# A typed graph-attention network on one core: table products on 32 rows, types loaded ahead, and the last part's orders skewed by groups

## The reference

```python
def gt_layer(x, ntype, etype, src, dst, Wk, Wq, Wv, Wa, Watt, Wmsg, pri, skip, g, b):
    k, q, v = (typed_linear(x, ntype, W).reshape(n, H, HS) for W in (Wk, Wq, Wv))
    kT = einsum('nhd,htdo->nhto', k, Watt)          # for every node, all 32 edge types
    vT = einsum('nhd,htdo->nhto', v, Wmsg)
    a = einsum('ehd,ehd->eh', kT[src, :, etype], q[dst]) * pri[:, etype].T / SQRT_D
    att = edge_softmax(a, dst, n)
    hag = segment_sum(vT[src, :, etype] * att[:, :, None], dst)
    h = silu(typed_linear(hag, ntype, Wa))
    alpha = sigmoid(skip[ntype])[:, None]
    return layernorm(h * alpha + x * (1.0 - alpha)) * g + b
h = x
for l in range(2): h = gt_layer(h, ...)
return layernorm(x + h @ ff_w + ff_b)
```

## Time and profile before

| | us |
|---|---|
| median of 3 runs | 6708.48 (6702.58 to 6715.25) |
| the profiled execution | 6708.81 |
| its span, first to last instruction | 6707.0 |
| table stage of layer 0, first to last copy | 518.5 to 1209.7 |
| table stage of layer 1, first to last copy | 3427.2 to 4220.0 |
| last part | 6394 to 6707 |

### The profile page before, as it was taken

The page is one execution under the profiler, slowest core; times in us unless marked ns, Lnnn a source line. Parts: engine busy times, 40 slices in busy tenths (PEclk is TensorE's granted clock), DMA queues, the critical chain, the costliest instruction groups (busy, mean ns, idle before and its releaser), DMA issues. The chain is left out here.

```text
span 6707.0 us, 77358 instructions
## 1 busy us (share of the span) xinstructions
PE 4184.1 (62%) x19359; PEld 2998.1 (45%) x19360; DVE 3641.0 (54%) x6709; ACT 1684.7 (25%) x4067; POOL 4108.6 (61%) x4128
## 2 busy tenths in 40 slices
PE   0208888666666666666368888666666666666344
PEld 0102223465555555555323333455565555556323
DVE  1304444566666666666545444566666666666634
ACT  0004444211111111111235444222222222222234
POOL 0463334677777777777324443677777777777553
PEclk9559999766776776677679999777766766676655
DMA  2317787466666666666446676566666666666310
GB/s 69 53 38 281 305 331 323 133 186 190 185 183 184 184 186 186 188 185 185 121 164 277 268 283 278 142 184 185 183 188 186 186 187 184 184 186 185 101 35 21
DMA packets 437457, 1224.41 MB, mean 183 GB/s; under 512 B 169857, under 2 KB 223109, under 8 KB 362224
## 3 DMA queue, kind: packets, MB, share of 16 engines
q0 software_dynamic: 233776, 852.10, 39.7%
q1 hardware_dynamic: 147104, 152.21, 10.7%
q10 hardware_dynamic: 56448, 218.59, 8.4%
HBM read 576.25 MB, written 718.61 MB: 193 GB/s over the span
## 5 line engine op out<-in xcount | busy, mean ns | idle before, releaser
L990 POOL DMA_INDIRECT kv_e<-table_d,row_s x1568 | 1545.2, 985 | 489.0 <-issue 485.3
L990 POOL DMA_INDIRECT kv_e_<-table_d,row_s_ x1568 | 1541.2, 983 | 487.2 <-issue 483.2
L1159 PE MATMUL sum_ps<-pv,to_rank 128*128 128x136 f32 x3136 | 610.9, 380 | 149.6 <-DVE pv L1077 149.6
L1159 PE MATMUL sum_ps_<-pv_,to_rank_ 128*128 128x136 f32 x3136 | 610.2, 379 | 149.0 <-DVE pv_ L1077 149.0
L1159 PEld LDWEIGHTS sum_ps<-pv,to_rank 128*128 128x128 f32 x3136 | 591.6, 284 | 177.8 <-issue 177.8
L1159 PEld LDWEIGHTS sum_ps_<-pv_,to_rank_ 128*128 128x128 f32 x3136 | 591.0, 283 | 177.2 <-issue 177.2
L1125 PE MATMUL qe_ps_<-q_w_,of_rank_ 128*128 (+1 forms) x3168 | 537.7, 328 | 148.2 <-DVE kq_ L1056 117.6
L1125 PE MATMUL qe_ps<-q_w,of_rank 128*128 (+1 forms) x3168 | 536.3, 328 | 147.8 <-DVE kq L1056 116.8
L1125 PEld LDWEIGHTS qe_ps_<-q_w_,of_rank_ 128*128 128x128 f32 x3168 | 470.2, 230 | 205.6 <-issue 197.7
L1056 DVE TENSOR_TENSOR kq_<-kv_e_,qe_ps_ 128x512 f32<-128x512 f32 x392 | 268.3, 684 | 540.5 <-DMA kv_e_<-table_d,row_s_ 540.1
L1056 DVE TENSOR_TENSOR kq<-kv_e,qe_ps 128x512 f32<-128x512 f32 x392 | 268.3, 685 | 539.2 <-DMA kv_e<-table_d,row_s 538.3
(11 more groups left out here) (376 smaller groups left out, 6666.7 us busy)
## 6 DMA issues: line engine op xcount, KB each, us to landing
part_d<-sums ACTq DMA_DIRECT2D x98, 1088.0 KB, 4.7
part_d<-sums_ ACTq DMA_DIRECT2D x98, 1088.0 KB, 4.7
local_b<-local_d SPq DMA_DIRECT2D x100, 512.0 KB
local_b_<-local_d SPq DMA_DIRECT2D x100, 512.0 KB
kv_e<-table_d,row_s POOLq DMA_INDIRECT x1568, 2.8
kv_e_<-table_d,row_s_ POOLq DMA_INDIRECT x1568, 2.8
q_w<-q_d SPq DMA_DIRECT2D x100, 64.0 KB
q_w_<-q_d SPq DMA_DIRECT2D x100, 64.0 KB
```

What stands on the lines that cost most here:

```text
L990: pool.indirect_dma_start(out=kv_e[:, b, t, :], out_offset=None, in_=table_d, in_offset=bass.IndirectOffsetOnAxis(ap=row_s[:, b, t:t + 1], ...
L1159: last = pe.matmul(sum_ps[:, n % 3, (t - t0) * REC:(t - t0 + 1) * REC], to_rank[:, b, t, :], pv[:, b, t, :], start=True, stop=True)
```

## The change

- **Table products.** `edge_w` is now as wide as 32 rows. A unit is two heads of sixteen edge types: still 512 columns and 16 matmuls a tile. PE issues them four at a time (K and V of two units), each on its own quarter of the rows and in its own bank. Units 0 to 3 fill pieces 0 and 1, units 4 to 7 pieces 2 and 3. So POOL scatters 0 and 1 after unit 3 and 2 and 3 after unit 7, and the copies wait before unit 0 for pieces 0 and 1 of the tile before, and before unit 4 for pieces 2 and 3. `turn_h` now stands in front of unit 0, the type loads and `turn` in front of unit 2, `multiply_h` in front of unit 4, `turn_kv` and the update's `multiply` in front of unit 6.
- **Types.** `load_types` loads the two types of a tile, one tile ahead in layer 0 and eight in layer 1, and the registers serve both products.
- **Last part.** Each engine's loop runs over steps i, and takes each operation for its own group i - d. The gathered sums have four buffers (`ring`) and the product by type two PSUM banks (`banks`). Stores run nine groups behind.
- A clear of 102 semaphores now also follows layer 1, since both Updates share their semaphores.

```diff
+    def load_types(pe, k):
+        return [pe.value_load(block_t[0:1, 2 * k + b:2 * k + b + 1], min_val=0, max_val=NT - 1) for b in range(2)]
...
-        edge_w = sb(st, "edge_w", [P, 2, RT, HALF])
+        edge_w = sb(st, "edge_w", [P, 2, RT, ROWS])
...
+            def unit(a, i):
+                at = ((a + i // 2) % 2 + i % 2 * 2) * ROWS
+                return slice(at, at + ROWS), slice(i // 4 * (RT // 2), (i // 4 + 1) * (RT // 2))
...
-                        pool.wait_ge(s_kc, (n * NPC + q + 1) * 2)
-                        pool.wait_ge(s_vc, (n * NPC + q + 1) * 2)
+                        pool.wait_ge(s_kc, n * UNITS + (q // 2 + 1) * 4)
+                        pool.wait_ge(s_vc, n * UNITS + (q // 2 + 1) * 4)
...
+                rows, ts = unit(a, i)
+                qs = slice(i // 4 * 2, i // 4 * 2 + 2)
+                if i % 4 == 0 and landed + n:
+                    for q in range(qs.start, qs.stop):
+                        eng.wait_ge(s_piece[q], landed + 16 * n)
...
-        if l < L - 1:
-            clear([name for name in sems if name not in prep_sems | keep])
+        clear([name for name in sems if name not in prep_sems | keep])
...
-    up = Update(st, "f", nd)
+    up = Update(st, "f", nd, 4, 2)
...
+            for i in range(NGP + 6):
+                if i < NGP:
+                    up.turn(pe, i)
+                    for k in range(i * GP, (i + 1) * GP):
+                        types[k] = load_types(pe, k)
+                if 0 <= i - 4 < NGP:
+                    turn_h(i - 4)
+                if 0 <= i - 1 < NGP:
+                    up.multiply(pe, i - 1, types)
...
+                if 0 <= i - 5 < NGP:
+                    multiply_h(i - 5)
...
+            for i in range(NGP + 8):
+                if 0 <= i - 1 < NGP:
+                    up.squash(act, i - 1)
+                if i < NGP:
+                    up.copy_turned(act, i)
+                if 0 <= i - 4 < NGP:
+                    copy_h(i - 4)
+                if 0 <= i - 2 < NGP:
+                    up.root(act, i - 2)
+                if 0 <= i - 6 < NGP:
+                    root(i - 6)
+                if 0 <= i - 3 < NGP:
+                    up.norm(act, i - 3)
+                if 0 <= i - 7 < NGP:
+                    norm_y(i - 7)
...
+            for i in range(NGP + 8):
+                if 0 <= i - 2 < NGP:
+                    up.gate(dve, i - 2)
+                if i < NGP:
+                    up.normalise(dve, i)
+                if 0 <= i - 6 < NGP:
+                    sums(i - 6)
+                if 0 <= i - 2 < NGP:
+                    up.invert(dve, i - 2)
+                if 0 <= i - 3 < NGP:
+                    up.scale(dve, i - 3)
+                if 0 <= i - 6 < NGP:
+                    invert(i - 6)
```

More of the change, by code:

```diff
@@ L822, in _ @@
             def _(pe):
+                types = {}
+                early = (LEAD + 1) * GP - 1 if up else 1
+                for k in range(early):
+                    types[k] = load_types(pe, k)
                 if up:
@@ L859, in fill @@
-            def fill(eng, copy, a, n, g, bank, s, s_copied):
-                q, rows = g // 2, half_of(a, g)
-                if g % 2 == 0 and landed + n:
-                    eng.wait_ge(s_piece[q], landed + 16 * n)
-                eng.wait_ge(s, n * (RT // TG) + g + 1)
-                copy(piece[:, q, :, a * D + rows.start:a * D + rows.stop],
-                     bank[:, g % 2, :].rearrange("p (t o) -> p t o", t=TP)).then_inc(s_copied, 1)
+                            pe.wait_ge(s_pri, u // 2 * 2 + 2)
@@ new lines, in fill @@
+            def fill(eng, copy, a, n, i, bank, s, s_copied):
+                rows, ts = unit(a, i)
+                qs = slice(i // 4 * 2, i // 4 * 2 + 2)
+                if i % 4 == 0 and landed + n:
+                    for q in range(qs.start, qs.stop):
+                        eng.wait_ge(s_piece[q], landed + 16 * n)
+                eng.wait_ge(s, n * UNITS + i + 1)
+                copy(piece[:, qs].rearrange("p q t f -> p (q t) f")[:, :, a * D + rows.start:a * D + rows.stop],
+                     bank[:, i % 2, :].rearrange("p (t o) -> p t o", o=ROWS)).then_inc(s_copied, 1)
@@ L1377, in _, with turn_h @@
         def _(pe):
-            def finish(g):
+            def turn_h(g):
                 pe.wait_ge(up.s_done, g + 1)
```

202 lines of the change are left out of this document (87 added, 115 removed).

## The result

The change makes the kernel slower: 6773.36 us (median of 4 runs, 6764.05 to 6774.95) against 6706.55 (4 runs, 6702.58 to 6715.25), a ratio of 1.010 with a 95% interval of 1.0088 to 1.0112. The prediction was 6686 us, a gain; the result lies at the upper end of its range (6625 to 6775) and has the other sign.

A forecast was written before the change was run, and what follows sets the result against it. Tables seemed bound by PE, the last part by a chain of waits; after the change, landings would bind the tables. Layer 0 -30, layer 1 -71, clock +8, last part +64, other +6: -23, so 6686 us, range 6625 to 6775.

The forecast's parts named there:

- So the second half binds: Layer 0 table: the wait of unit 4 for pieces 2 and 3 sets the tile, 11.65 us, 11.85 with jitter.
- the landing of 4.9 us: Table tile: time from piece 3's issue to its landing, with nothing ahead of it, used in the 11.65 us cycle.
- +8 us: Both tables: cost allowed for a lower TensorE clock, a tenth of the four copies' growth from 3.34 to 4.2 us.
- 91 us as the bad end: Both tables: cost if the clock falls to 0.50 throughout, 106 tiles at 0.86 us each.
- as forecast (2 to 3): Layer 0 table: VectorE's copy of unit 4 would wait some 2 to 3 us a tile for DMA.
- PE's share: Table stages: PE's busy share would fall to about 65%, idling 2.7 us a tile before unit 6.
- -71 forecast: Layer 1 table: a gain of 71 us, with update tiles at 13.1 us instead of 14.30.
- forecast as nearly gone: Table stage: the 163.8 us PE waits on "issue" before the products by type would nearly vanish.
- I give the packing itself nothing: Tables: four 32-row products at once gain nothing, since the bank's round trip (1.21 + 0.69 us) sets the unit.
- +64 forecast: Last part: a loss of 64 us, each step a closed loop of 17.9 us against 14.72.
- -91 forecast: Both tables together: layer 0 -28 us, layer 1 -71, and +8 for the clock.
- landing takes more: Rival for the tables: piece 3 lands in 6.0 us, cycle 12.75, whole kernel 6780 us; chance 0.22.

The follow-up runs named there:

- x5b: The change with the buffer `piece` doubled, so copies wait for the landing of the tile before the last: tables 585.9 and 668.2 us, ratio 0.9732.
- x11: Tables of 64-row products with types loaded ahead, plus both couplings: copies wait for two pieces, scatters go in pairs; ratio 1.0198 against the kernel before.
- x14: Tables of 64-row products with types loaded ahead, plus only the copies' wait for two pieces' landings: layer 0 635.8 us, layer 1 670.0, ratio 0.9729.
- x15: Tables of 64-row products with types loaded ahead, plus only the scatters held until two pieces are filled: layer 0 636.8 us, layer 1 677.9, ratio 0.9745.
- x4: The change with 12 unread products added on TensorE in each tile of both tables: 724.2 and 792.5 us, ratio 1.0146 against the kernel before.
- x10: The change's table packing and coupled waits alone, types loaded between products and last part as before: tables 724.1 and 885.9 us, ratio 1.017.
- x3: The change with TensorE's products put ahead of the new group's turn and type loads in the last part: 270.5 us there, ratio 0.997.
- x7: 64-row tables as before the change, with types loaded ahead and the last part's products first: 6423.93 us against 6708.73, ratio 0.9567.
- x9: The change with `piece` doubled and the last part's products ahead of the turn and type loads: tables 585.5 and 676.3 us, ratio 0.9672.
- x12: The change with `piece` doubled, the last part's products first and 12 unread products added a tile: tables 669.9 and 787.0 us, ratio 0.9911.
- x8: 64-row tables with types loaded ahead, the last part's products first and `piece` doubled: 6425.80 us, ratio 0.9571 against the kernel before.
- x1: The change's two tables kept, with the last part set back to that of the kernel before: last part 312.7 us, ratio 1.0029.

## Why the prediction was wrong

- **Layer 0, the step that failed: "So the second half binds", 11.65 us a tile.** That the copies would wait for landings was right, and the second half's loop exists as I drew it (11.64 us in the tile shown). But I gave it the landing of 4.9 us, and I took pieces 0 and 1 for done. What the runs showed is two loops of about one length through one DMA queue, of which now one binds and now the other, in 12.8 us a tile. My sum issued pieces 0 and 1 at 4.6 and 5.9, which supposes that their filling starts at once, and let them land at 13.5, so that the next filling starts 1.9 late; with that delay in front of the fill, and the 6.2 us of the earlier trace rows for the second of a pair, their loop is 3.34 + 0.78 + 1.27 + 6.2 = 11.6, level with the 11.65. Measured are 3.77 + 0.87 + 1.27 + 6.87 = 12.78: 0.43 more to fill and 0.67 more from the second issue to the next copy. Where a landing ends the second half's wait, the copy starts 5.5 us behind piece 3's issue, not 4.9. x5b shows what the landing waits cost, 136 us; x11, x14 and x15 show that it takes both halves of the coupling to cost so much.
- **The clock in it.** The filling takes 3.19 us at a granted clock of 1.00 and some 4.15 at 0.50, so the clock is part of a loop that binds, and part of the 0.43. In x4, at 0.93 for the stage, the tile is as long, with longer landing waits. So "+8 us" and "91 us as the bad end" are neither confirmed nor refuted: what the fallen clock costs by itself stays open.
- **The budget of a tile.** VectorE's landing waits, 150.4 / 57 = 2.64 us a tile, came as forecast (2 to 3), but its waits for products are 277.2 / 57 = 4.86 where 11.65 left 3.4. In x4 these are 3.17, and the landing waits rise to 4.38: the sum stays. PE's share was forecast at 65% and is 599.90 / 721.70 = 83%: it idles where I said, but its products take longer at the lower clock.
- **Layer 1: -71 forecast, -20.4 found,** 13.86 a tile, not 13.1. Here the loop of pieces 0 and 1 is nearly alone: a landing ends the wait of 42 of 47 next-tile starts, and the filling takes 5.3 us. The gain of the types ahead did come, 113 us by x10; the landing waits, 104 us by x5b, stood against it.
- **The type loads.** Right in part: a load fell to 300 ns, but of the 163.8 us of "issue", forecast as nearly gone, 92.8 are left. Missed was what this part alone is worth, 81 and 129 us, since the table with separate waits had no landing to wait for.
- **The packing.** "I give the packing itself nothing" was near: 22 us in layer 0 with the loops open, none in layer 1. The 3.07 times of "TensorE: Matmul & The Clock Gate" (the Trainium skill, "Part 3: Packing small matmuls — row/col tiling") does not show here: a tile of layer 0 with the loops open takes 10.4 us with it and 10.7 without.
- **The last part: +64 forecast, +50.5 found.** The mechanism and its order held (tanh waiting for PE, scale for norm, the table load in the open). The round is 17.0 us and not 17.9; six loads take 3.50 and not 3.9; the first seven steps are shorter than the round. x3 shows that the order makes the loop.
- **The sum.** Of the 78 us between forecast and profile (-23 and +55.2), 101 are the tables' (-91 forecast, +10.1 found); the last part came out 14.5 better than forecast and the other stretches 8.4. The rival "landing takes more" had 6780 us with 0.22, and its mechanism, pieces landing later with others close by, is the nearest to what happened, though it had only the second half's piece in it. That its 12.75 us a tile meets the measured 12.8 is partly luck, since some of the excess is in the filling. Its condition, tables that gain less than 70 us together, came true: they lose 10.

## What to carry to other kernels

When a change makes buffers share a wait, close every loop, not only the one that looks longest: fill, wait for the whole, issue, landing behind its neighbour, and back, each start fed by the last end. Here two loops came out level in the sum (11.6 us), and the tile was longer than either (12.8), in part by the clock. Landing times grew here by what was issued just ahead (4.9 us, then 6.2 for the second of a pair); use the figure of the second. And before you read a fallen clock as the cause, take its waits away: if it comes back by itself, it followed them.

## What was not expected of the hardware

- A register load takes 742 ns at the median between products by type and 300 ns in front of unit 2, in the same stage under the same DMA traffic (median of 110). So it is not the traffic of the stage as a whole. At the end of a tile's products, in x7, it takes 606. What makes the difference was not tested.
- The first step of the last part took 32.3 to 37.9 us in x3, x4, x9 and x11 to x15, and 7.3 and 11.6 in x7 and the change, with the same code for the steps (x3 and x7 alike). x3, x9, x12, x14 and x15 ended at 269 to 271 us, x7 and x8 at 238; the long step came only in sets where the edge stretches took some 2850 us, and there only with the new last part (x1 and x10, with the old one, step by 14.7 from the start). Its cause is open. In x3 it is ScalarE that stands still, ahead of its second tanh, and for nothing that the profile shows:

```profile
7770.73 0.49 ACT L655 ACTIVATE f_tanh_s<-f_lin_ps 128x384 f32<-128x384 f32 x1 [30.35 <-issue]
```
